# Routing of the second batch dealt out in small pieces between the shared FFN tiles, and its last tables among the expert slots

## The chip, the cores and the metric

The kernel runs on one core of a Trainium2 chip. The metric is the device time of one execution in microseconds (us), less is better. TensorE is the matrix engine (PE in the profile), VectorE is DVE, ScalarE is ACT, GpSimd is POOL, and SyncE (SP) issues most of the plain transfers.

## What is computed

One decoder layer in float32 over 32 sequences of 64 tokens, 2048 tokens of 256 features: linear attention, cross attention over a context, and a feed-forward part with 8 experts of which each token takes 2, beside a shared expert. Each has a layer norm before it and is added to x. The attention parts end before the stretch of this case; the feed-forward part is:

```python
logits = einsum('td,ed->te', xf, gate_w)
weights, indices = top_k(softmax(logits), 2)
weights = weights / weights.sum(-1, keepdims=True)
combine = einsum('tk,tke->te', weights, one_hot(indices, 8))
h = silu(einsum('td,edh->teh', xf, w_gate)) * einsum('td,edh->teh', xf, w_up)     # hidden size 176
out = einsum('teh,ehd,te->td', h, w_down, combine)
sh = silu(xf @ shw_gate) * (xf @ shw_up) @ shw_down                               # hidden size 352
out = out + sigmoid(xf @ shgate_w)[:, None] * sh
```

## The kernel before

Tokens are worked in 16 tiles of 128. A loop over the tiles carries both attention parts, the third layer norm and the router's logits. Behind it come three stages, all written out by hand in the order in which each engine does them; semaphores tie the engines together and nothing reorders.

*Shared tiles.* For tile t, TensorE turns the normalised input (transpose_sx), makes gate and up products (shared_gate, shared_up, six products each, since every float32 product is made of three passes on high and low parts), and later the transpose of the hidden row (transpose_sh, for tile t - 1) and the down product (shared_down, for tile t - 2). ScalarE makes the high part of the turned input (s_xh, L1214), the tanh of the gate (s_th, L1219) and the high part of the turned hidden row (s_hh, L1224 and L1225). VectorE makes (tanh + 1) * gate (s_gg, L1702), the low part of the *next* tile's input (s_xl, L1695), the hidden row s_h (L1709), its low part s_hl (L1718, L1720) and adds the down product to x (residual3, L1725). In VectorE's shared(t) they stand in this order, so the next tile's gate product hangs on s_gg of this one. Twelve tiles (EARLY_SHARED) are done before the experts and four behind them; the first three are mixed with the end of the attention.

*Routing.* It is done in two batches, tiles 0 to 10 and 11 to 15, called batch 1 and batch 2 here (0 and 1 in the code). VectorE finds the first choice (route_first, seven instructions), ScalarE takes the exponential (route_exp, L1134) and the shared gate's sigmoid (shared_gates), VectorE finds the second choice (route_rest, route_second), TensorE counts with a triangular and a full matrix of ones who comes before whom (ranks, four short products, L777), VectorE makes each token's row number (route_rows, L1563 to L1571) and its two weights (route_weights, L1547 to L1550), then where each expert's rows end (clear_rows, slot_counts) and a table of which expert and which first row each slot has (slot_table, L1607 to L1618). GpSimd's send scatters each token's row twice into a buffer in memory, xs_rows, sorted by expert; it waits for the row numbers of its batch and, tile by tile, for s_h of an earlier tile.

Each of these VectorE instructions is wrapped in chained(), which makes the next one wait for it.

*Expert slots.* The buffer is worked in 39 slots of 128 rows: 15 (FULL_SLOTS) that the first batch alone fills, and 24 whose table needs both batches. SyncE loads a slot's rows (load_slots) when the table of its part and that part's sends are there and slot i - 4 has been turned and given its output row numbers; TensorE reads the expert's number into a register (expert_of) and makes gate and up (gate_up), the transpose of the hidden row (L987), that of a later slot's input (L972) and down (expert_down). ScalarE and VectorE work as for shared tiles: e_th (L1283), e_gg (L1799), e_h (L1805), e_hl (L1810), xl (L1794). GpSimd scatters the results to y_rows, and at the end they are loaded, summed and stored.

VectorE's order around the change, before:

```python
            slot_table(0)
            shared(3)
            keep_logits(15)
            route_first(1)
            shared(4)
            route_rest(1)
            route_second(1)
            shared(5)
            route_rows(1)
            route_weights(1)
            clear_rows()
            shared(6)
            slot_counts(1)
            shared(7)
            slot_table(1)
```

## Time and profile before

| | |
|---|---|
| median of 3 runs | 391.13 us (389.28 to 392.36) |
| profiled execution, its own time | 389.04 us |
| its span, first to last instruction | 387.2 us |
| TensorE products, busy | 351.5 us (91%) |
| VectorE busy | 281.7 us (73%) |
| ScalarE busy | 219.5 us (57%) |
| GpSimd busy | 220.8 us (57%) |
| mean granted TensorE clock | 0.983 of full speed |

The profile is that of one execution, and its times count from the span's start. Products are pipelined and overlap, so their recorded lengths add to more than the time they take: the start of one against the start of the next tells what it costs. The shared tiles stand from about 205 to 272 us, the slots from there to 362.

### The profile page before, as it was taken

Reading aid. Unit: us, or ns where it says so; the run is one execution under the profiler, and the core shown is the slowest. Engines: PE = TensorE matmul, PEld = TensorE weight load, DVE = VectorE, ACT = ScalarE, POOL = GpSimd, SP = SyncE. Lnnn points to the kernel's source line nnn. Section 1 sums busy time; section 2 is a strip of 40 time slices with the busy share of each in tenths; the row PEclk is TensorE's granted clock in tenths of the full one; section 3 lists DMA queues with packets and bytes.
Section 4 is the critical chain, followed back from the end, with each engine's and each line's share of the span. In section 5 each row is a group of like instructions: output and inputs, shape, how many; then the busy total and the mean of one; then the engine's idle time right before and its main releaser. Section 6 shows DMA issues by size and latency. Waiting matters only on the chain.

```text
span 387.2 us, 12001 instructions
## 1 busy us (share of the span) xinstructions
PE 351.5 (91%) x3890; PEld 310.1 (80%) x3890; DVE 281.7 (73%) x922; ACT 219.5 (57%) x570; POOL 220.8 (57%) x262
## 2 busy tenths in 40 slices
PE   7789999999999999999986987998899999999971
PEld 5567778888888888888875876987788999999960
DVE  3757887788878888787886576985666767676574
ACT  3345677677776777767755333323355666665541
POOL 1247677876778766787656643544334444443362
PEclk9999999999999999999999699999999999999996
DMA  8922012211122201220000111214355343442297
GB/s 231 372 88 60 18 47 60 62 42 36 46 59 59 59 16 43 59 59 15 2 3 29 42 57 42 71 69 140 112 168 154 118 133 118 130 123 87 65 391 251
DMA packets 22013, 36.15 MB, mean 93 GB/s; under 512 B 2928, under 2 KB 15856, under 8 KB 21968
## 3 DMA queue, kind: packets, MB, share of 16 engines
q1 hardware_dynamic: 17984, 25.46, 21.6%
q0 software_dynamic: 3408, 9.39, 6.4%
q10 hardware_dynamic: 576, 0.72, 0.7%
q8 instruction: 25, 0.41, 0.4%
q14 instruction: 20, 0.16, 0.2%
HBM read 22.88 MB, written 12.69 MB: 92 GB/s over the span
## 4 chain that ended last, share of the span: by engine, by line
PE 61%; DVE 14%; ACT 9%; issue 6%; DMA 5%; another core or an unknown queue 1%; SPq 1%; POOL 1%; ACTq 1%; DVEq 0%; POOLq 0%
PE ps L851 22%; PE ps L748 4%; PE ps L666 3%; PE ps L695 3%; PE ps L720 3%; PE ps L628 3%; DMA yg<-y_rows 3%; PE ps L653 2%; PE ps L611 2%; PE ps L685 2%; PE ps L987 2%; PE ps L972 2%; ACT w_hi L1113 2%; PE ps L618 2%; ACT q L1064 2%
## 5 line engine op out<-in xcount | busy, mean ns | idle before, releaser
L578 POOL DMA_INDIRECT y_rows<-e_y,out_row x39 | 37.5, 962 | 48.2 <-ACT e_y L1294 46.1
L521 POOL DMA_INDIRECT xs_rows<-x_send,pos x32 | 31.2, 974 | 32.3 <-DVE s_h L1709 18.2
L504 POOL TENSOR_TENSOR w_lo<-w_stage,w_hi 128x852 f32 (+1 forms) x14 | 28.0, 2000 | 19.8 <-ACT w_hi L1113 18.7
L490 POOL TENSOR_TENSOR bias_t<-alibi,key_off 128x1024 f32<-128x1024 f32 x16 | 34.3, 2143 | 0.0
L497 POOL TENSOR_TENSOR sc<-sc,smax 128x1024 f32<-128x1024 f32 x16 | 30.5, 1905 | 6.6 <-DVE smax L1451 6.6
L1799 DVE SCALAR_TENSOR_TENSOR e_gg<-e_th,ps 128x176 f32<-128x176 f32 x39 | 13.2, 338 | 25.5 <-ACT e_th L1283 23.3
L851 PE MATMUL ps<-w_hi,xh 128*128 x78 | 27.2, 349 | 1.0 <-issue 0.5
L463 POOL TENSOR_TENSOR st<-mv,eps 128x1 f32<-128x1 f32 x32 | 7.0, 218 | 36.4 <-DVE mv L1434 23.5
L851 PE MATMUL ps<-w_hi,e_hh 88*128 x78 | 25.2, 323 | 1.0 <-DVE e_hl L1810 1.0
L851 PE MATMUL ps<-w_hi,s_xh 128*128 128x352 f32 x64 | 23.1, 361 | 3.0 <-DVE s_xl L1695 2.9
L1283 ACT ACTIVATE e_th<-ps 128x176 f32<-128x176 f32 x39 | 12.4, 318 | 23.2 <-PE ps L851 20.0
L851 PE MATMUL ps<-w_lo,xh 128*128 x78 | 25.2, 323 | 0.0
L851 PE MATMUL ps<-w_hi,xl 128*128 x78 | 25.2, 323 | 0.0
L1294 ACT ACTIVATE e_y<-ps,id_w 128x256 f32<-128x256 f32 x39 | 18.6, 476 | 11.2 <-PE ps L851 9.5
L851 PE MATMUL ps<-w_lo,e_hh 88*128 x78 | 21.9, 280 | 0.0
L851 PE MATMUL ps<-w_hi,e_hl 88*128 x78 | 21.9, 280 | 0.0
L1445 DVE TENSOR_TENSOR sc<-ps,bias_t 128x1024 f32<-128x1024 f32 x16 | 19.5, 1219 | 2.2 <-remote 2.2
L851 PE MATMUL ps<-w_hi,s_xl 128*128 128x352 f32 x64 | 21.0, 328 | 0.0
L851 PE MATMUL ps<-w_lo,s_xh 128*128 128x352 f32 x64 | 21.0, 328 | 0.0
L748 PE MATMUL ps<-xw_last,o2T 128*128 128x256 f32 x64 | 18.9, 420 | 2.0 <-ACT o2T L1095 0.6
L1451 DVE TENSOR_REDUCE smax<-sc 128x16 f32<-128x1024 f32 x16 | 19.5, 1220 | 0.5
L1219 ACT ACTIVATE s_th<-ps 128x352 f32<-128x352 f32 x16 | 7.4, 461 | 21.4 <-PE ps L851 16.4
(234 smaller groups left out, 1203.7 us busy)
## 6 DMA issues: line engine op xcount, KB each, us to landing
w_stage<-in_w_ffn_dram SPq DMA_DIRECT2D x14, 426.0 KB, 3.4
xs<-xs_rows SPq DMA_DIRECT2D x39, 130.5 KB
yg<-y_rows SPq DMA_DIRECT2D x8, 512.0 KB, 7.6
ctxT<-in_ctxT_dram SPq DMA_DIRECT2D x16, 128.0 KB, 2.1
out_dram<-x_all SPq DMA_DIRECT2D x7, 256.0 KB, 4.5
x_all<-in_x_dram SPq DMA_DIRECT2D x1, 1280.0 KB, 11.0
xs_rows<-zeros SPq DMA_DIRECT2D x9, 130.5 KB, 6.9
y_rows<-e_y,out_row POOLq DMA_INDIRECT x39
```

Source lines behind the costliest of these rows:

```text
L490: nc.gpsimd.tensor_tensor(bias_t[:, :].rearrange("p (h k) -> p h k", h=HEADS), alibi[:, :].rearrange("p (h k) -> p h k", h=HEADS), ko, ALU ...
L497: nc.gpsimd.tensor_tensor(v, v, spread(smax[:, :].rearrange("p (h o) -> p h o", o=1), 2, S), ALU.subtract).then_inc(sm["sub_ready"], 1)
L504: nc.gpsimd.tensor_tensor(w_lo[:, cols], w_stage[:, half, :], w_hi[:, cols].bitcast(F32), ALU.subtract).then_inc(sm["w_lo_ready"], 1)
L521: nc.gpsimd.indirect_dma_start(out=xs_d[:, :], out_offset=bass.IndirectOffsetOnAxis(ap=pos[:, t, r:r + 1], axis=0), in_=x_send[:, t, :], i ...
L578: nc.gpsimd.indirect_dma_start(out=y_d[:, :], out_offset=bass.IndirectOffsetOnAxis(ap=out_row[:, i:i + 1], axis=0), in_=e_y[:, q, :], in_o ...
L748: mm = T.matmul(ps[:, A3, 0:D], o2T[:, k, :], xwo[:, k, :], start=(k == 0), stop=(k == KC - 1))
L851: mm = T.matmul(out_ap, lhs, rhs[rows, cols], start=st, stop=en)
L1283: A.activation(e_th[:, p, :], ps[:, EG + p, 0:H], ACT.Tanh, scale=0.5).then_inc(sm["e_th_ready"], 1)
L1294: A.activation(e_y[:, q, :], ps[:, ED + q % 2, 0:D], ACT.Copy, scale=id_w[:, i, 1:2]).then_inc(sm["e_y_ready"], 1)
L1445: V.tensor_tensor(sc[:, :].rearrange("p (j c) -> p j c", j=4), ps[:, B0:B3 + 1, 0:256], bias_t[:, :].rearrange("p (j c) -> p j c", j=4), A ...
L1451: V.tensor_reduce(smax[:, :], sc[:, :].rearrange("p (h k) -> p h k", h=HEADS), AX.X, ALU.max).then_inc(sm["smax_ready"], 1)
L1799: V.scalar_tensor_tensor(out=e_gg[:, p, :], in0=e_th[:, p, :], scalar=1.0, in1=ps[:, EG + p, 0:H], op0=ALU.add, op1=ALU.mult).then_inc(sm[ ...
```

## The change

On VectorE the routing of batch 2 is dealt out in ten pieces instead of five. Four functions are cut in two: route_first gives off route_hot (the last three instructions), route_rows gives off rows_before (the first three), slot_counts gives off slot_jumps (the last two, three in batch 2), slot_table gives off slot_rows (the last four, five in batch 2). The pieces stand one between each two shared tiles, and the last three behind expert slots 4, 6 and 8. For batch 1 the pieces stand together as they did, but for slot_rows(0), which goes behind shared(3). On ScalarE route_exp(1) and shared_gates(1) move from ahead of shared(4) to behind shared(6), on TensorE ranks(1) from tile 5's end to tile 8's. No instruction is added or dropped.

```diff
@@ TensorE, shared tiles
-                if t == DRAIN_SHARED + 2:
+                if t == 8:
                     ranks(1)
@@ ScalarE
             shared_x_high(4, 0)
-            route_exp(1)
-            shared_gates(1)
             for t in range(DRAIN_SHARED + 1, EARLY_SHARED):
                 shared(t, DRAIN_SHARED, EARLY_SHARED)
+                if t == 6:
+                    route_exp(1)
+                    shared_gates(1)
@@ VectorE, the cut of route_first as an example of the four
                 chained(V.tensor_reduce(top_e, is_top, AX.X, ALU.max))
+
+            def route_hot(b):
+
+                T, n = tiles_of(b)
+                top, top_e = choice(b, "top"), choice(b, "top_e")
                 chained(V.tensor_tensor(hot[:, 0, T, :], by_expert(top_e), by_tile(rev8[:, :], n), ALU.is_equal))
@@ VectorE, shared tiles
             slot_table(0)
             shared(3)
             keep_logits(15)
+            slot_rows(0)
+            shared(4)
             route_first(1)
-            shared(4)
+            shared(5)
+            route_hot(1)
+            shared(6)
             route_rest(1)
             route_second(1)
-            shared(5)
+            shared(7)
+            route_weights(1)
+            shared(8)
+            rows_before(1)
+            shared(9)
             route_rows(1)
-            route_weights(1)
             clear_rows()
-            shared(6)
+            shared(10)
             slot_counts(1)
-            shared(7)
-            slot_table(1)
-            for t in range(8, EARLY_SHARED):
-                shared(t)
+            shared(11)
             v.wait_ge(sm["sg4_ready"], 2)
@@ VectorE, expert slots
             for i in range(1, SLOT_TILES):
                 experts(i)
+                if i == 4:
+                    slot_jumps(1)
+                if i == 6:
+                    slot_table(1)
+                if i == 8:
+                    slot_rows(1)
```

In the rows below, line numbers are each kernel's own: in the changed one s_gg is L1724, s_xl L1717, s_h L1731, e_gg L1827, e_h L1833, and the routing lines lie 1 to 21 further down.

VectorE around shared tile 3, before (ge, row_jump, row and row_i are table 0's second half, lg is keep_logits(15), tops and row_x open batch 2's first choice):

```order
L1610 TENSOR_SCALAR slot_rev<-slot_e 128x15
L1611 TENSOR_TENSOR ge<-ge,jump 128x120
L1612 TENSOR_REDUCE row_jump<-ge 128x15
L1616 SCALAR_TENSOR_TENSOR row<-consts,row_jump 128x15
L1618 TENSOR_SCALAR row_i<-row 1x15
L1702 SCALAR_TENSOR_TENSOR s_gg<-s_th,ps 128x352
L1695 TENSOR_TENSOR s_xl<-ps,s_xh 128x256
L1709 SCALAR_TENSOR_TENSOR s_h<-s_gg,sg,ps 128x352
L1485 COPY lg<-ps 128x9
L1518 TENSOR_REDUCE tops<-lg 128x5
L1519 TENSOR_TENSOR row_x<-lg,tops 128x40
L1520 TENSOR_TENSOR row_x<-row_x,consts 128x40
```

The same place in the changed kernel:

```order
L1625 TENSOR_SCALAR slot_rev<-slot_e 128x15
L1724 SCALAR_TENSOR_TENSOR s_gg<-s_th,ps 128x352
L1717 TENSOR_TENSOR s_xl<-ps,s_xh 128x256
L1731 SCALAR_TENSOR_TENSOR s_h<-s_gg,sg,ps 128x352
L1486 COPY lg<-ps 128x9
L1632 TENSOR_TENSOR ge<-ge,jump 128x120
L1633 TENSOR_REDUCE row_jump<-ge 128x15
L1637 SCALAR_TENSOR_TENSOR row<-consts,row_jump 128x15
L1639 TENSOR_SCALAR row_i<-row 1x15
L1724 SCALAR_TENSOR_TENSOR s_gg<-s_th,ps 128x352
L1717 TENSOR_TENSOR s_xl<-ps,s_xh 128x256
L1731 SCALAR_TENSOR_TENSOR s_h<-s_gg,sg,ps 128x352
```

The second half of the table now stands behind s_h of tile 3, and tile 4's s_gg comes next instead of batch 2's first choice.

ScalarE ahead of tile 4's tanh, before (L1134 is the exponential of batch 2, sgt and sg the shared gate):

```order
L1122 ACTIVATE xn3T<-ps 128x256
L1214 ACTIVATE s_xh<-ps 128x256
L1134 ACTIVATE pe<-lgs 128x40
L1141 ACTIVATE sgt<-lg 128x5
L1143 ACTIVATE sg<-sgt,quarter 128x5
L1219 ACTIVATE s_th<-ps 128x352
```

And in the changed kernel:

```order
L1122 ACTIVATE xn3T<-ps 128x256
L1214 ACTIVATE s_xh<-ps 128x256
L1219 ACTIVATE s_th<-ps 128x352
L1214 ACTIVATE s_xh<-ps 128x256
L1224 ACTIVATE s_hh<-ps 128x256
L1225 ACTIVATE s_hh<-ps 96x128
L1219 ACTIVATE s_th<-ps 128x352
```

The tanh of tile 4 stands directly behind the input copy of tile 4; the three routing instructions come three tiles later.

VectorE behind expert slot 4 in the changed kernel (before, e_gg of slot 5 follows second at once):

```order
L1838 TENSOR_TENSOR e_hl<-ps,e_hh 88x256
L1822 TENSOR_TENSOR xl<-ps,xh 128x256
L1845 TENSOR_TENSOR second<-xs,slot_rev 128x1
L1602 SCALAR_TENSOR_TENSOR cum<-ones,til 128x8
L1603 SCALAR_TENSOR_TENSOR jump<-til,consts 128x8
L1606 SCALAR_TENSOR_TENSOR jump<-taken_step,jump 128x8
L1827 SCALAR_TENSOR_TENSOR e_gg<-e_th,ps 128x176
```

Three small instructions of batch 2 now stand between slot 4's last work and slot 5's first; four and five more stand likewise behind slots 6 and 8.

## Rows read from the trace of the kernel before

A timeline row reads: start us, us, engine, line, operation, out<-in, forms, count, and in brackets the engine's idle time before it with its releaser.

**Rows 1.** The chain that ended last, routing stretch: start us, us, engine, name, line

```profile
238.76 1.25 issue
240.01 0.34 DVE s_gg L1702
```

**Rows 2.** TensorE's timeline, first gate product of shared tiles 4, 5, 9, 10

```profile
236.81 0.43 PE L851 MATMUL ps<-w_hi,s_xh 128*128 128x352 f32 x1 [0.65 <-DVE s_xl L1695]
...
240.93 0.43 PE L851 MATMUL ps<-w_hi,s_xh 128*128 128x352 f32 x1 [1.38 <-DVE s_xl L1695]
...
256.98 0.43 PE L851 MATMUL ps<-w_hi,s_xh 128*128 128x352 f32 x1 [0.70 <-DVE s_xl L1695]
...
260.62 0.33 PE L851 MATMUL ps<-w_hi,s_xh 128*128 128x352 f32 x1
```

**Rows 3.** VectorE's timeline, 234.9 to 258.8 us: where each piece of routing begins and ends

```profile
234.98 0.28 DVE L1611 TENSOR_TENSOR ge<-ge,jump 128x120 f32<-128x120 f32 x1
...
235.91 0.51 DVE L1702 SCALAR_TENSOR_TENSOR s_gg<-s_th,ps 128x352 f32<-128x352 f32 x1
...
237.35 0.20 DVE L1518 TENSOR_REDUCE tops<-lg 128x5 f32<-128x40 f32 x1
...
241.81 0.18 DVE L1530 SCALAR_TENSOR_TENSOR pe<-hot,pe 128x40 f32<-128x40 bf16 x1
...
243.07 0.52 DVE L1702 SCALAR_TENSOR_TENSOR s_gg<-s_th,ps 128x352 f32<-128x352 f32 x1
...
245.19 0.16 DVE L1563 COPY counts<-upto 128x8 f32<-128x8 f32 x1
...
246.79 0.16 DVE L1547 TENSOR_SCALAR tops<-tops 128x5 f32<-128x5 f32 x1
...
247.57 0.50 DVE L1702 SCALAR_TENSOR_TENSOR s_gg<-s_th,ps 128x352 f32<-128x352 f32 x1
...
249.69 0.41 DVE L1581 TENSOR_SCALAR cnt_i<-upto 128x8 int32<-128x8 f32 x1
...
250.95 0.18 DVE L1587 TENSOR_TENSOR_SCAN cum<-ones,til 128x8 f32<-128x8 f32 x1
...
251.57 0.52 DVE L1702 SCALAR_TENSOR_TENSOR s_gg<-s_th,ps 128x352 f32<-128x352 f32 x1
...
253.69 0.34 DVE L1607 TENSOR_TENSOR ge<-consts,cum 128x192 f32<-128x192 f32 x1
...
254.77 0.36 DVE L1611 TENSOR_TENSOR ge<-ge,jump 128x192 f32<-128x192 f32 x1
...
256.07 0.51 DVE L1702 SCALAR_TENSOR_TENSOR s_gg<-s_th,ps 128x352 f32<-128x352 f32 x1
...
258.74 0.52 DVE L1702 SCALAR_TENSOR_TENSOR s_gg<-s_th,ps 128x352 f32<-128x352 f32 x1 [0.47 <-ACT s_th L1219]
```

**Rows 4.** ScalarE's timeline, copy of tile 4 and the exponential of batch 2

```profile
235.15 0.38 ACT L1214 ACTIVATE s_xh<-ps 128x256 fp32r<-128x256 f32 x1
238.96 0.24 ACT L1134 ACTIVATE pe<-lgs 128x40 f32<-128x40 f32 x1 [3.43 <-DVE lgs L1524]
```

**Rows 5.** Windows, one expert slot: length, then PE, PEld, DVE, ACT, POOL busy, PEclk

```profile
288.35:290.45 2.10, 2.10 (x18) 2.06 (x17) 1.51 (x7) 1.34 (x5) 0.81 (x2) 1.00 0.61 190
```

**Rows 6.** VectorE's and TensorE's timelines, h of slot 5 and its transpose

```profile
286.48 0.33 DVE L1805 SCALAR_TENSOR_TENSOR e_h<-e_gg,ps 128x176 f32<-128x176 f32 x1
...
287.80 0.38 PE L987 MATMUL ps<-ident,e_h 128*88 128x128 f32 x2
```

**Rows 7.** VectorE's and ScalarE's timelines, end of the shared tiles

```profile
269.36 0.42 DVE L1725 TENSOR_TENSOR x_all<-ps,x_all 128x256 f32<-128x256 f32 x1 [1.25 <-PE ps L851]
...
269.41 0.39 ACT L1278 ACTIVATE xh<-ps 128x256 fp32r<-128x256 f32 x1 [1.95 <-PE ps L972]
```

**Rows 8.** TensorE's timeline at 213 us, and the window behind it (columns of rows 5)

```profile
213.27 0.41 PE L756 MATMUL ps<-ident,xn 128*128 128x128 f32 x2 [3.21 <-DVE sc L1445]
...
215.00:220.00 5.00, 5.00 (x19) 4.64 (x20) 2.00 (x7) 1.06 (x1) 4.29 (x6) 0.50 0.15 53
```

More of the change, by code:

```diff
@@ L1551, in route_weights, with rows_before @@
                                 ).then_inc(sm["fields_ready"], 1)
-            def route_rows(b):
+            def rows_before(b):
                 T, n = tiles_of(b)
@@ L1557, in route_rows @@
                 ranks = ps[:, RANKS[b], :]
-                in_tile, row = rows_scratch(b, "in_tile"), rows_scratch(b, "row")
+                in_tile = rows_scratch(b, "in_tile")
                 by_tiles = in_tile.rearrange("p (e t) -> p e t", e=NE)
@@ L1566, in route_rows @@
                                              not_first[b][:, :, :].rearrange("p e t -> p (e t)"), in_tile, 0.0, ALU.mult, ALU.add))
+            def route_rows(b):
+                T, n = tiles_of(b)
+                counted = n * NE
+                ranks, row = ps[:, RANKS[b], :], rows_scratch(b, "row")
                 chained(V.tensor_tensor(row.rearrange("p (t e) -> p t e", e=NE), ranks[:, 0:counted].rearrange("p (t e) -> p t e", e=NE),
@@ L1610, in slot_table, with slot_rows @@
                 chained(V.tensor_scalar(slot_rev[:, I], slot_e[:, 0:n], -1.0, float(NE), ALU.mult, ALU.add))
+            def slot_rows(b):
+                i0, n = ((0, FULL_SLOTS), (FULL_SLOTS, SLOT_TILES - FULL_SLOTS))[b]
+                I = slice(i0, i0 + n)
+                iota, g = iota_slot[:, 0:n], ge[:, 0:n, :]
                 chained(V.tensor_tensor(g, g, by_tile(jump[:, :], n), ALU.mult))
@@ L1642, in body @@
                     route_first(0)
+                    route_hot(0)
                 if has(t, 0):
@@ L1738, in _ @@
             shared_x_low(0, 0)
+            rows_before(0)
             route_rows(0)
@@ L1759, in _ @@
             slot_counts(0)
+            slot_jumps(0)
             sh_low(1, 1, A2)
```

1 line of the change is left out of this document (added).

## The prediction

> **What bounds the kernel now.** I read the page first, for which engine is busy and the granted clock, then the chain that ended last to see where the end is not held by TensorE, then the timelines of TensorE and VectorE side by side there, and last the windows by expert slot.
>
> Over most of the span TensorE sets the end. The exception that this change touches is the shared FFN with the routing of batch 2. There the chain runs instruction by instruction through VectorE, and TensorE comes in only now and then; between batch 2's first routing piece and the next shared tile it shows 1.25 us in which VectorE waits [rows 1]. The first gate product of a shared tile marks when TensorE begins it. Tile 4 begins at 236.81, tile 5 at 240.93, tile 9 at 256.98, tile 10 at 260.62 [rows 2]. From 9 to 10, with no routing between, a tile takes 3.64 us and TensorE has no gap: that is its own pace, gate, up, down and transposes together. Tile 4 took 4.12 though it has no down product yet, and tiles 5 to 8 together 256.98 - 240.93 = 16.05, which is 1.49 more than four times 3.64. Each marked gap waits for s_xl, the low part of the next tile's input, which VectorE makes behind s_gg of the current tile.
>
> What stands ahead of those s_gg is the routing. On VectorE the second half of table 0 runs from 234.98 to 235.91, batch 2's first choice from 237.35 until ScalarE gets its input at 238.96 [rows 4], the second choice from 241.81 to 243.07, ranks, rows and weights from 245.19 to 247.57, the counts with their jumps from 249.69 to 251.57, the table from 253.69 to 256.07 [rows 3]. VectorE's own work on a tile is 256.07 to 258.74 less the 0.47 it waited, 2.20 us [rows 3]. A tile of 3.64 thus leaves VectorE 1.44 us. The table alone is 2.38 us, the ranks with the weights 2.38, the counts with the jumps 1.88: too long for one gap, and TensorE waits for the rest.
>
> **Where it is hidden and where not.** Two lengths say how large a piece may be. s_gg of tile 9 begins 1.76 after tile 9's first product (258.74 - 256.98), and the next tile's first product comes 0.90 after s_gg begins (236.81 - 235.91), so the chain product, tanh, s_gg, s_xl, product closes in 2.66 us. Against 3.64 that is 0.98 of play for one late piece, and the 1.44 bounds what may come in every gap.
>
> **The change, part by part.**
>
> 1. Table 0's second half (four instructions, 0.93 us) moves from ahead of shared tile 3 to behind it. s_gg of tile 3 can begin 0.93 earlier. ScalarE's copy for tile 4 ends at 235.15 + 0.38 = 235.53 [rows 4]; s_xl follows, and TensorE can begin tile 4 0.47 after that if the 0.43 between s_gg and s_xl is taken off 0.90. That gives 236.00 instead of 236.81: gain 0.8, between 0 and 0.93. What reads the moved half is the load of slot 0, and that also waits until the first batch is sent, whose last send waits for s_h of tile 8; so the delay costs nothing.
>
> 2. The first choice is cut in two, and the exponential moves on ScalarE from ahead of the tanh of tile 4 to behind tile 6. Before, that tanh stood behind an exponential that waited 3.43 us for lgs [rows 4], which is the 1.25 us of rows 1. Without it tile 4 has the closed chain of 2.66 us instead of 4.12: gain 1.46. The lower bound is 4.12 - 3.64 = 0.48, should tile 4 go at the pace of the others; I take 1.46, since there is no down product in it. What is late next is TensorE itself.
>
> 3. The rest is dealt out one piece to a gap. By the starts in rows 3: ranks with their rows 1.60 (now in two gaps, about 0.7 and 0.9), weights 0.78 with the end rows, second choice 1.26, counts without the jumps 1.26. Every one is under 1.44, so tiles 5 to 8 should fall to TensorE's pace: gain 1.49, less about 0.1 (an estimate) for the four short rank products, which stay in the stretch, now behind tile 6's down product. The bounds are 0 and 1.49. The rank products wait for nothing any more: the one-hot rows are ready two tiles earlier in the new order. Behind them on TensorE stands tile 9's gate, and VectorE's ranks piece comes behind shared tile 8, so a wait there would need them over a tile late.
>
> 4. Behind it: the row numbers of batch 2 (pos) now come after tile 9 instead of after tile 5. GpSimd's sends of tile 11 wait for s_h of tile 9 anyway, and now also for the rows piece, about 1 us behind it. Its two sends have a tile of 3.64 for themselves. No cost. The clearing of the ends needs them only among the slots.
>
> 5. Among the expert slots: three instructions behind slot 4 (0.62), then the nine of the table, four behind slot 6 and five behind slot 8 (by that share about 1.1 and 1.3), 3.00 in all [rows 3]. A slot takes 2.10 us, and VectorE is busy 1.51 of it [rows 5]: 0.59 free. h of slot 5 is done at 286.48 + 0.33 = 286.81 and its transpose on TensorE begins at 287.80 [rows 6], 0.99 later. So a piece of up to 0.59 + 0.99 = 1.58 us is hidden once, if the next slots give it back at 0.59 each; the largest is 1.30, and two slots lie between the pieces. The last one is close, since not all of the piece before it may have been given back. Bounds 0 and 3.00 us; I take 0.15, near the rows that show it hidden. Nobody waits for the table itself: the first load of a slot of the second part waits for the row numbers of slot 11, which VectorE makes behind all three pieces, and TensorE reads the slot's expert later still.
>
> The sum against the profiled execution: 0.8 + 1.46 + 1.39 = 3.65 gained, 0.15 given back, 3.5 us. That execution took 389.04 with a span of 387.2, and would take 385.5. From slot 0 on TensorE sets the end, so what it arrives earlier is kept. The median of the three runs is 391.13, 2.1 over the profiled one; I take the difference over to the median: 391.13 - 3.5 = 387.6 us. All bounds taken against me, 0.48 is left of the gain in the tiles and 3.00 is paid in the slots: 2.5 slower; all for me, 0.93 + 1.46 + 1.49 = 3.9 faster.
>
> **The rivals.**
>
> *The pieces cost in full among the slots.* If TensorE is tied among the slots to e_gg, the counterpart of s_gg, the 3.00 us stand in its way: gain 3.65 - 3.00 = 0.65, 390.5 us. For it: VectorE has only 0.59 us free a slot against 1.44 in a shared tile. Against it: the 0.99 us by which h is early.
>
> *A late signal goes or comes.* At the end of the shared tiles VectorE and ScalarE go on within 0.05 us of each other, at 269.36 and 269.41, after 1.25 and 1.95 us of waiting for TensorE products whose recorded end is 1.4 us earlier [rows 7]. If that stall belongs to a place in the program it stays. If it belongs to what else happens to move at that time, shifting everything by 3.5 us can remove it: 1.4 more gained, 386.2 us. It can as well come up elsewhere. On fetching of instructions the Trainium skill, "Runtime: NRT & Kernel Launch", section "Instruction fetch mechanics", says that an engine draws its instructions ahead in blocks and that crossing from one to the next is mostly hidden. By that rule the stall is no property of the place and might go, which is the 386.2; the trace doesn't say which it is.
>
> *A burst meets a stall and the clock falls* (the slower side). Earlier in the trace TensorE idled 3.21 us, and in the 5 us behind the granted clock was 0.50, the 1.2 GHz level [rows 8]. If one of the pieces behind slots 4, 6 or 8 meets a stall like that of rows 7, the two add: 1.3 + 1.95 is about as long an idle time. It would cost that 3.2 and half of 5 us at the lower level, 5.7 in all: 5.7 - 3.65 = 2.1 slower, 393.2 us. It decides from the point where TensorE stands idle for some 3 us at once.
>
> **How the numbers follow.** The forecast has 0.61, the pieces paid in full 0.20, the vanished signal 0.13, the fallen clock 0.06. The range goes from 385.2, below the vanished signal's time, to 390.8, just past the pieces paid in full; it leaves out most of the clock case and the tails. 1% is 3.9 us, about what a measurement of this kernel tells from no change (the three runs lie within 0.8%). The forecast lies just short of that bound, so I give 0.28 of its 0.61 to faster by over 1%, and nearly all of the vanished signal's: 0.40. Slower by over 1% is a corner of the clock case, 0.03. Within 1% is the rest, 0.57.
>
> **What would show it.** Right: first gate products of tiles 5 to 9 about 3.64 us apart, tile 9's at 253.3 or so in place of 256.98; no wait for s_xl at TensorE in those tiles; the tanh of tile 4 behind its own gate product and not behind the exponential; slots 5 to 10 at 2.1 to 2.4 us each as before, and slot 0's first product 3.6 earlier. Wrong: a gap at TensorE behind slot 8 that ends with e_h or e_hl, a rank product that waits for hot, GpSimd's sends of batch 2 holding up the loads from slot 15 on, or tiles that stay above 3.7 us with VectorE never idle, which would mean that a piece costs more than its start-to-start time.

## The result, and the profile after

In the first comparison the changed kernel took **392.21 us** (median of 13 runs, 389.33 to 394.06) beside 389.92 us for the kernel before (13 runs, 388.40 to 392.36). The ratio is **1.0053, 95% interval 1.0031 to 1.0074**: 0.5% slower, where the prediction had 387.6 us. By the bound of 1% this is no change; the time lies above the predicted range. The profiled execution took 390.13 us, the second fastest of the 13, and the slower executions have the lower mean clock (389.33 us with 0.978 of full speed, 394.06 with 0.964). So the trace shows 1.1 us of the difference in span, where the medians differ by 2.3. Three executions of later comparisons (399.31 us, 485.55 and 659.75) were in a slow state: they count in the medians printed here, but not in the ratios.

Three lines of the page of the changed kernel, first comparison: the span, the clock granted to TensorE in 40 slices, and the chain that ended last by engine.

```profile
span 388.3 us, 12003 instructions
...
PEclk9999999999999999999999799998999999999995
...
PE 68%; ACT 9%; DVE 7%; issue 7%; DMA 3%; another core or an unknown queue 3%; POOL 2%; DVEq 0%; ACTq 0%; POOLq 0%; SPq 0%
```

There is a second dip in the clock row (slice 28), and 3% of the chain is put down to "another core", though this program has one core. Both matter below. TensorE's timeline of the same execution (start, duration, engine, line, operation; in brackets the idle time before and its releaser) answers to [rows 2]: the first gate products of tiles 4, 5, 8, 9 and 10, then the transposes of slots 0 and 1, the down product of shared tile 10, and slot 0's first product.

```profile
234.95 0.43 PE L851 MATMUL ps<-w_hi,s_xh 128*128 128x352 f32 x1
...
237.62 0.43 PE L851 MATMUL ps<-w_hi,s_xh 128*128 128x352 f32 x1
...
249.62 0.43 PE L851 MATMUL ps<-w_hi,s_xh 128*128 128x352 f32 x1 [1.10 <-DVE s_xl L1717]
...
253.38 0.41 PE L851 MATMUL ps<-w_hi,s_xh 128*128 128x352 f32 x1
...
257.63 0.43 PE L851 MATMUL ps<-w_hi,s_xh 128*128 128x352 f32 x1 [0.46 <-DVE s_xl L1717]
...
264.60 0.60 PE L972 MATMUL ps<-ident,xs 128*128 128x128 f32 x4
...
269.77 0.46 PE L851 MATMUL ps<-w_hi,s_hh 128*128 128x256 f32 x1 [4.57 <-DVE x_all L1747]
...
272.23 0.64 PE L851 MATMUL ps<-w_hi,xh 128*128 x1
```

Tile 4 takes 2.67 us as forecast (2.66), and tile 9 begins at 253.38 instead of 256.98, 3.6 us earlier, as forecast. The sum agrees better than its terms: tiles 5 to 8 take 15.76 us here in place of 16.05, a gain of 0.29 where 1.39 was forecast, and tile 4 begins 1.86 earlier where 0.8 was. Later TensorE stands idle for 4.57 us, and slot 0 begins at 272.23, where it was 271.32 in the kernel before: everything that was won is lost there, and 0.9 us more. The same down product in the kernel before:

```profile
269.94 0.36 PE L851 MATMUL ps<-w_hi,s_hh 128*128 128x256 f32 x1 [1.56 <-DVE x_all L1725]
```

The idle time is 3.01 us longer in the changed kernel. From that product to slot 0 it takes 2.46 us instead of 1.38. VectorE's and ScalarE's timelines answer to [rows 7]. VectorE:

```profile
264.95 0.58 DVE L1731 SCALAR_TENSOR_TENSOR s_h<-s_gg,sg,ps 128x352 f32<-128x352 f32 x1 [1.43 <-PE ps L851]
...
269.20 0.42 DVE L1747 TENSOR_TENSOR x_all<-ps,x_all 128x256 f32<-128x256 f32 x1 [1.70 <-remote]
```

ScalarE:

```profile
262.44 0.47 ACT L1219 ACTIVATE s_th<-ps 128x352 f32<-128x352 f32 x1 [1.50 <-issue]
266.31 0.39 ACT L1224 ACTIVATE s_hh<-ps 128x256 fp32r<-128x256 f32 x1 [3.40 <-remote]
...
269.25 0.66 ACT L1279 ACTIVATE xh<-ps 128x256 fp32r<-128x256 f32 x2 [2.39 <-remote]
```

xh at 269.25 reads the transposes that began at 264.60 and had ended by 265.20: 4.05 us late. x_all at 269.20 reads a down product that ended at 264.76, 4.44 us late. ScalarE and VectorE go on within 0.05 us of each other, as they did in [rows 7], where the lateness was 1.4 us. "remote" says that the trace holds no event of this core that released them. I call such a case a late signal. That is a name for the row and not a cause: the ends of products are modelled in the profile, so the trace doesn't tell a signal that was late from a product that was. In this trace there are five such episodes behind 230 us (at 240, 247, 255, 264 to 269 and 278 to 280 us) against three in the kernel before (262, 268 to 271 and 277 to 280). Behind the longest of them the clock falls. Windows of the changed kernel (columns of [rows 5]):

```profile
266.00:268.00 2.00, 0.00 (x0) 0.00 (x0) 0.61 (x2) 0.54 (x2) 1.70 (x2) 1.00 0.31 111
...
270.00:272.00 2.00, 2.00 (x11) 2.00 (x11) 0.64 (x5) 0.00 (x0) 0.00 (x0) 0.50 0.00 0
272.00:274.00 2.00, 2.00 (x10) 1.76 (x9) 1.18 (x5) 0.58 (x3) 0.00 (x0) 0.68 0.00 0
```

The granted clock is 0.50, the 1.2 GHz level, in 270 to 272 and partly in 272 to 274: as in [rows 8], after TensorE had stood idle. That is why the stretch from the down product to slot 0 is 1.08 us longer. From slot 0 to the gate products of the last slot the changed kernel loses 1.3 us more (359.14 against 356.92). What GpSimd does in those microseconds is six sends, 0.30 to 0.47 us of pause between them; the first and the last:

```profile
260.56 0.96 POOL L521 DMA_INDIRECT xs_rows<-x_send,pos  x1 [5.18 <-issue]
...
267.07 0.96 POOL L521 DMA_INDIRECT xs_rows<-x_send,pos  x1 [0.30 <-issue]
```

They are one row because batch 2's row numbers come only behind tile 9 now (the prediction's step 4). In both traces each episode behind 230 us went with four or more sends 1.3 to 1.6 us apart; the episode at 209 to 213 us went with two. That rows of sends make signals late was my first theory, called A in the expectations.

### The profile page after: what moved, and what is told of

Same layout as the page of the kernel before. It is cut to its first block, busy times and chain, and to the rows that moved or that the text cites. A ratio compares the mean times of both kernels' runs of the same rounds, so it can differ in the third digit from the quotient of the medians.

```text
span 388.3 us, 12003 instructions
## 1 busy us (share of the span) xinstructions
PE 353.5 (91%) x3890; PEld 312.3 (80%) x3890; DVE 281.3 (72%) x922; ACT 219.4 (56%) x570; POOL 221.2 (57%) x262
## 4 chain that ended last, share of the span: by engine, by line
PE 68%; ACT 9%; DVE 7%; issue 7%; DMA 3%; another core or an unknown queue 3%; POOL 2%; DVEq 0%; ACTq 0%; POOLq 0%; SPq 0%
PE ps L851 25%; PE ps L748 4%; PE ps L666 4%; PE ps L720 4%; PE ps L695 3%; PE ps L628 3%; PE ps L611 3%; PE ps L653 2%; PE ps L685 2%; PE ps L987 2%; PE ps L972 2%; PE ps L618 2%; PE ps L615 2%; ACT w_hi L1113 2%
## 5 line engine op out<-in xcount | busy, mean ns | idle before, releaser
L1827 DVE SCALAR_TENSOR_TENSOR e_gg<-e_th,ps 128x176 f32<-128x176 f32 x39 | 13.2, 338 | 22.9 <-ACT e_th L1284 18.4
L851 PE MATMUL ps<-w_hi,s_hh 128*128 128x256 f32 (+1 forms) x48 | 16.4, 341 | 6.9 <-DVE x_all L1747 6.0
```

Source lines behind the costliest of these rows:

```text
L851: mm = T.matmul(out_ap, lhs, rhs[rows, cols], start=st, stop=en)
L1827: V.scalar_tensor_tensor(out=e_gg[:, p, :], in0=e_th[:, p, :], scalar=1.0, in1=ps[:, EG + p, 0:H], op0=ALU.add, op1=ALU.mult).then_inc(sm[ ...
```

## The experiments

The experiments ran in six comparisons, each with the kernel before on the same chip. They name their chips: 11 (the first four runs), 12 (the next four), 10 (two comparisons), 2 and 4 (the stalls). The first comparison names none, so I can't say whether its chip was one of these at another hour.

### Four tests of the sends

**The kernel before with its sends bunched.** The odd tiles' sends wait for one h more:

```diff
-                    pool.wait_ge(sm["s_h_ready"], t - 1)
+                    pool.wait_ge(sm["s_h_ready"], t if t % 2 and t < 10 else t - 1)
```

> The kernel before, with one edit: GpSimd's two sends of an even tile (from tile 5 on) wait as before, those of an odd tile for one s_h more, so that the four sends of two tiles come in one row. Theory A (a row of four or more sends, 1.27 us apart, goes with TensorE signals that reach ScalarE and VectorE 1 to 4 us late; what was won in the changed kernel was lost so): new late signals near the end of each row in the shared tiles, 1 to 2 us of idle TensorE for each, 2 to 6 us slower than before. Rival B (the late signals belong to something else, instruction fetching or the place in the program): late signals stay at 263 and 268 us as in the kernel before and none are added; within 1 us of before. Rival C (the loss in the changed kernel is VectorE's routing pieces): within 1 us of before as well.

**The kernel before with sends spaced.** In send(), inside the loop over the two rows:

```diff
                        in_=x_send[:, t, :], in_offset=None).then_inc(sm[f"sent{b}"], 16)
+                    if t >= 4:
+                        nc.gpsimd.tensor_tensor(pad[:, 2 * t + r:2 * t + r + 1], eps[:, :], neg_half[:, :], ALU.pow)
```

> The kernel before, with a small GpSimd operation of 0.57 us on a spare buffer behind each send from tile 4 on: sends are at least about 1.9 us apart instead of 1.27. Theory A (rows of sends make the late signals): the late signals of 263, 268 to 270.8 and 277 to 280 us go; 1 to 3 us faster than before, or the lateness shrinks with the spacing. Rival B (not the sends): they stay, and the time with them, within 1 us. A middle result (rows at 1.9 us still bring some) would show as smaller lateness at the same places.

**The changed kernel with the same edit.**

> The changed kernel with the same small GpSimd operation behind each send. Theory A: the late signals at 240, 247, 255 and 264 to 269 us go or shrink, tiles 5 to 11 stay at 3.64 us, slot 0 starts about 3 us earlier than before, no clock at half speed near 270 us; 3 to 5 us faster than the changed kernel and 1 to 4 us faster than before. Rival B (not the sends): as the changed kernel, 2 us slower than before, with the idle 4.6 us in front of slot 0. Rival D (the pieces among the slots are paid in full, 3 us): the shared tiles gain, but the slots from 5 on take 3 us more than before, sum within 1 us of before.

**The changed kernel with batch 2's row numbers one tile earlier:**

```diff
-                if t == 8:
+                if t == 7:
                     ranks(1)
...
             route_weights(1)
-            shared(8)
             rows_before(1)
-            shared(9)
+            shared(8)
             route_rows(1)
             clear_rows()
+            shared(9)
             shared(10)
```

> The changed kernel with the rank products one tile earlier and the pieces behind them as well, so that the row numbers of batch 2 are there one tile earlier; the pieces behind shared tile 7 are two then. Theory A: the sends of tiles 11 to 13 come no longer six in a row but in pairs or fours, the idle 4.6 us in front of slot 0 shrinks to 1 to 2 us and the clock does not fall behind it: 2 to 4 us faster than the changed kernel. Rival B (not the sends): no difference to the changed kernel but that of a larger piece behind tile 7, 0 to 0.5 us slower.

Measured: 1.0082 (1.0055 to 1.0110), 1.0023 (1.0001 to 1.0046), 0.9973 (0.9949 to 0.9997) and 0.9893 (0.9865 to 0.9922), all against the kernel before, which took 383.68 us here and not 389.92. The first of the four did more than I meant: in its trace ten sends stand in one row. GpSimd's timeline of the kernel with bunched sends, the first and the last of the ten:

```profile
253.72 0.95 POOL L521 DMA_INDIRECT xs_rows<-x_send,pos  x1 [3.73 <-DVE s_h L1709]
...
265.06 0.96 POOL L521 DMA_INDIRECT xs_rows<-x_send,pos  x1 [0.30 <-issue]
```

and ScalarE's, in the midst of them:

```profile
259.32 0.38 ACT L1224 ACTIVATE s_hh<-ps 128x256 fp32r<-128x256 f32 x1 [0.77 <-PE ps L893]
...
261.37 0.47 ACT L1219 ACTIVATE s_th<-ps 128x352 f32<-128x352 f32 x1 [1.50 <-PE ps L851]
```

s_hh is in time behind its transposes, with the same 0.77 us of waiting as in quiet tiles, and s_th follows its gate product in 0.04 us. So theory A as I had stated it is refuted on this chip: rows of sends don't make late signals by themselves. None of these four traces has a late signal among the shared tiles. The bunched kernel is 0.8% slower, within what theory A had forecast, but for another and plainer reason: its sends come later, and TensorE waits for rows of slots 0 and 1 (0.59 and 0.87 us, released by the DMA of xs). The spacing costs something too (the third run is 3 us above the unspaced kernel of the next comparison) and cures nothing, since here nothing is late. What these runs say of a chip with late signals is nothing.

### Both kernels again, unchanged

> The kernel before, unchanged, for a profile from the chip of this comparison (the earlier profiles of both kernels may come from another). Theory E (the late TensorE signals belong to the chip or to the hour, not to the order of the program): if this chip shows none, the span is some 381 to 382 us, 5 below the 387.2 of the first profile, and the difference lies at 209 to 212, 262 to 271 and 277 to 280 us. Theory A (rows of sends make them): late signals at the rows of four sends, as in the first profile.

> The changed kernel, unchanged, on the chip of this comparison. Theory E: without late signals the change gives what its steps promise, 3 to 4 us (the variant with the row numbers a tile earlier gave 4.2), gate products of tiles 5 to 11 3.64 us apart, slot 0 some 3.5 us earlier, no half clock near 270 us. Theory A: slower than before by 2 us, with rows of four to six sends and late signals behind them, the idle 4.6 us and the half clock, as in its first profile. Rival F (the row numbers of batch 2 come too late and this costs by itself): 2 to 4 us slower than the variant with them a tile early, and no late signal seen.

The kernel before against itself: 383.83 us, 1.0001 (0.9982 to 1.0020). The changed kernel: **379.90 us, ratio 0.9889 (0.9865 to 0.9913)**. A third copy on another chip gave 379.34 us and 0.9885 (0.9857 to 0.9912):

> The changed kernel unchanged, to tell what kind of chip this comparison ran on. Theory E (what turns the sign is the chip: one with late signals or one without): before near 383.7 us goes with a ratio of about 0.989, before near 390 us with one of about 1.005, and nothing between. Were the first verdict a chance of the kernel's own scatter instead, the ratio would fall between these.

Theory E holds as far as it could be tried: before at 383.6 to 384.1 us goes with a change that is 1.1% faster. Its other half, before near 390 us with a ratio of 1.005, is the first comparison alone. TensorE's timeline of the kernel before on this chip (first gate products of tiles 4, 5 and 9, and slot 0's first product):

```profile
233.65 0.43 PE L851 MATMUL ps<-w_hi,s_xh 128*128 128x352 f32 x1 [0.64 <-DVE s_xl L1695]
...
237.76 0.43 PE L851 MATMUL ps<-w_hi,s_xh 128*128 128x352 f32 x1 [1.37 <-DVE s_xl L1695]
...
253.82 0.43 PE L851 MATMUL ps<-w_hi,s_xh 128*128 128x352 f32 x1 [0.70 <-DVE s_xl L1695]
...
266.54 0.41 PE L851 MATMUL ps<-w_hi,xh 128*128 x1
```

and of the changed kernel (tiles 4, 5, 6, 9 and 10, then the down product that was 4.57 us late in the first trace, and slot 0's first product):

```profile
232.63 0.43 PE L851 MATMUL ps<-w_hi,s_xh 128*128 128x352 f32 x1
...
235.31 0.43 PE L851 MATMUL ps<-w_hi,s_xh 128*128 128x352 f32 x1
...
238.97 0.33 PE L851 MATMUL ps<-w_hi,s_xh 128*128 128x352 f32 x1
...
249.71 0.41 PE L851 MATMUL ps<-w_hi,s_xh 128*128 128x352 f32 x1
...
253.35 0.33 PE L851 MATMUL ps<-w_hi,s_xh 128*128 128x352 f32 x1
...
261.03 0.36 PE L851 MATMUL ps<-w_hi,s_hh 128*128 128x256 f32 x1 [0.20 <-DVE x_all L1747]
...
262.41 0.41 PE L851 MATMUL ps<-w_hi,xh 128*128 x1
```

The idle time in front of the down product is 0.20 us in place of 4.57. Side by side, changed minus before:

| place | first comparison | chip 12 |
|---|---|---|
| tile 4 begins | 234.95 - 236.81 = -1.9 | 232.63 - 233.65 = -1.0 |
| tile 9 begins | 253.38 - 256.98 = -3.6 | 249.71 - 253.82 = -4.1 |
| slot 0 begins | 272.23 - 271.32 = **+0.9** | 262.41 - 266.54 = **-4.1** |
| span | 388.3 - 387.2 = +1.1 | 378.6 - 383.3 = -4.7 |

The profiled execution of the kernel before took 385.22 us here, 1.4 over its median, so the span row overstates the gain; the medians give 3.8. Read along a kernel, the first comparison is ahead of chip 12 up to the first send at 209 us, by 0.9 us in the kernel before and 1.2 in the changed one; from there it is late. The kernel before is 3.2 us later at tile 4 and 4.8 at slot 0; the changed one is 2.3 us later at tile 4, 3.7 at tile 9 and 9.8 at slot 0. This also explains [rows 8]: the idle time of 3.21 us with the half clock behind it was itself a late signal. In the traces of chip 12 the same product waits 1.04 us, and the window behind it has full clock. The clock doesn't hang on this idle time alone, though: in three other traces (the kernel before with spaced sends, the changed one with its row numbers a tile earlier, and the second run of paired sends) the same wait is 1.02 to 1.03 us, and the granted clock is 0.50 from 214 to 216 us. The window of the changed kernel on chip 12:

```profile
214.00:219.00 5.00, 4.45 (x33) 4.14 (x31) 3.28 (x11) 2.27 (x4) 3.79 (x6) 1.00 0.15 53
```

In this execution of the changed kernel the six sends of tiles 11 to 13 stand in one row as well, from 255.65 to 262.93, and ScalarE's timeline shows no harm from them:

```profile
260.64 0.66 ACT L1279 ACTIVATE xh<-ps 128x256 fp32r<-128x256 f32 x2 [0.74 <-PE ps L972]
```

The same instruction had come 4.05 us late in the first trace.

### The prediction's steps one by one

**Pieces among the slots undone** (jumps and table of batch 2 behind tile 10, slot rows behind tile 11, nothing among the slots):

```diff
             slot_counts(1)
+            slot_jumps(1)
+            slot_table(1)
             shared(11)
+            slot_rows(1)
...
-                if i == 4:
-                    slot_jumps(1)
-                if i == 6:
-                    slot_table(1)
-                if i == 8:
-                    slot_rows(1)
```

> The changed kernel with the pieces among the expert slots put back: jumps and table of batch 2 behind shared tile 10, its slot rows behind tile 11, nothing among the slots. By the prediction's step 5 the pieces among the slots cost 0.15 (0 to 3.0): then this is equal to the changed kernel or 0 to 1 us slower, as the table's 2.4 us stands in the way of the last shared tiles. Rival D (paid in full among the slots): 1 to 3 us faster than the changed kernel.

379.99 us, 0.9902 (0.9872 to 0.9931), beside 379.90 for the changed kernel: no difference. From slot 0 to slot 11 it takes 26.85 us where the changed kernel takes 27.04, but its slot 0 begins at 263.89, 1.5 later. The 0.19 us is no price of the pieces. Two traces of the changed kernel differ by more (27.04 and 26.59), and in this one the clock fell at slot 0:

```profile
262.24 0.36 PE L851 MATMUL ps<-w_hi,s_hh 128*128 128x256 f32 x1 [1.84 <-DVE x_all L1747]
...
264.00:266.00 2.00, 2.00 (x7) 2.00 (x8) 1.39 (x7) 0.45 (x2) 0.00 (x0) 0.50 0.18 67
```

Slot 0 took 3.77 us with it in place of 2.85. What can be said is that the pieces cost far less than the 3.00 us that they are long: slots 5 to 9, among which they stand, take 11.49 and 11.69 us in two traces of the changed kernel, 12.44 with the pieces undone and 12.00 in the kernel before.

**Large pieces kept, steps 1 and 2 alone:**

```diff
-            route_first(1)
-            shared(5)
-            route_hot(1)
-            shared(6)
...
+            route_first(1)
+            route_hot(1)
+            shared(5)
+            route_rest(1)
+            route_second(1)
+            shared(6)
...
```

(and so on: ranks, rows and weights behind tile 6, counts and jumps behind 7, the whole table behind 8; the exponential at tile 5).

> The changed kernel with steps 1 and 2 kept (table 0's second half behind tile 3, the exponential off tile 4's way) and step 3 and 5 undone: batch 2's routing behind tiles 4 to 8 in the old large pieces, nothing among the slots. By the prediction's sum: 0.8 + 1.46 stay, 1.4 of the tiles is lost: 2.2 us faster than before (ratio 0.994) where no signal is late; first gate products of tiles 5 to 10 above 3.64 us apart, by the length of the piece. Were the gain one of fewer waits for signals rather than of piece size, it would be near the 3.8 us of the whole change. On a chip like that of the first two profiles (before at 389 to 390 us) theory A lets the rows of sends decide: the sends of tile 11 come earlier here than in the change, so 1 to 3 us faster than before.

381.37 us, 0.9917 (0.9886 to 0.9948): 3.2 us faster than before with a wide interval, where 2.2 was expected; the clock time can't separate these. The trace does: tile 4 takes 2.68 us as in the change, and tiles 5 to 9 take 3.64, 3.71, 4.12, 4.01 and 4.50, so together they take 1.9 us more than the changed kernel's 18.04. In the shared tiles the pieces' size and place are worth that.

**Batch 2's routing one tile earlier all through** (a try for something better):

```diff
+            slot_counts(1)
             shared(10)
-            slot_counts(1)
+            slot_jumps(1)
             shared(11)
...
-                if i == 4:
-                    slot_jumps(1)
-                if i == 6:
+                if i == 4:
                     slot_table(1)
-                if i == 8:
+                if i == 6:
                     slot_rows(1)
```

(on top of the fourth run above).

> The changed kernel with batch 2's routing one tile earlier all through: weights and end rows behind tile 7, row numbers behind tile 8, counts behind 9, jumps behind 10; among the slots only the table behind slot 4 and the slot rows behind slot 6. It aims at the gap in front of slot 11, 3.3 us in the changed kernel where its neighbours take 2.1 to 2.3 (the first slot whose rows wait for batch 2). If that gap hangs on the sends and slot rows of batch 2: it falls to 2.2 to 2.5 us, 0.5 to 1.5 us faster than the changed kernel, ratio to before 0.985 to 0.989. If it hangs on something else: as the changed kernel, within 0.5 us, or up to 1 us slower where a piece no longer fits. On a chip like that of the first two profiles (before at 389 to 390 us) theory A expects it 2 to 4 us faster than the changed kernel, since no six sends come in a row.

379.07 us, 0.9872 (0.9841 to 0.9904), beside 379.34 us for the changed kernel in the same comparison: no difference that can be measured. The gap in front of slot 11 (3.29 us in the changed kernel of chip 12) stayed at 3.25 here, and in the third copy of the changed kernel it was 2.78. TensorE's row at slot 11 in the changed kernel of chip 12 names the DMA of the slot's rows:

```profile
287.92 0.44 PE L972 MATMUL ps<-ident,xs 128*128 128x128 f32 x2 [0.32 <-DMA xs<-xs_rows]
```

so there TensorE waits for the load. That the slot rows are what holds the load up isn't shown: two slots earlier they changed nothing. The gap was 2.20 us in the first of the stalls below, with VectorE's order unchanged. What sets it stays open.

**Earlier rows and spaced sends together**, and **pairs of sends kept apart** (two small operations behind each pair instead of one behind each send), the latter on two chips:

> The changed kernel with both edits: row numbers of batch 2 one tile earlier, and the small GpSimd operation behind each send. If spacing the sends and the earlier rows help apart from each other: 1 us or more below the variant with the earlier rows alone (ratio to before about 0.986). If the spacing only costs GpSimd time where no signal is late: 0 to 1 us above it (0.989 to 0.992).

> The changed kernel with two small GpSimd operations (0.57 us each) behind each pair of sends from tile 4 on: pairs stay at 1.27 us, but no more than two sends are in a row. On a chip like that of the runs before this one (before at 383.7 us, no late signals): 0 to 2 us slower than the changed kernel, as in the variant with one operation behind each send, since GpSimd gets later with batch 2. On a chip like that of the first two profiles (before at 389 to 390 us): theory A expects the late signals of 240, 247, 255 and 264 to 269 us gone and 3 us or more off the changed kernel; if they stay, rows of sends are not what makes them there either.

> The changed kernel with pairs of sends kept apart, as in the run before with this name's pairs. Where before takes about 384 us and no signal is late: a ratio of 0.992 as there. Where before takes about 390 us, theory A: a ratio of 0.985 to 0.995 instead of the 1.005 of the changed kernel, late signals at 240, 247, 255 and 264 to 269 us gone. If the ratio is 1.00 or more and they stay: rows of sends do not make them.

0.9962 (0.9942 to 0.9983), 0.9918 (0.9880 to 0.9955) and 0.9962 (0.9930 to 0.9993). On chips where nothing is late the spacing costs 1 to 3 us, more than I had expected in the first and the last of the three; it was to cure what these chips don't have.

### What an idle time in front of slot 0 costs

No comparison met a chip with late signals again, so I made the idle time in the changed kernel, with N small activations ahead of ScalarE's copy of the h of tile 10:

```diff
+                if t == 11:
+                    for j in range(N):
+                        A.activation(pad[:, j:j + 1], quarter[:, :], ACT.Copy)
                 if t - 1 >= first:
                     sh_high(t - 1, (t - 1) % 2)
```

> The changed kernel with nine small activations (some 0.2 us each, 1.8 in all) ahead of ScalarE's copy of the h of shared tile 10, so that TensorE stands idle in front of slot 0 for about 2 us more. If an idle time there is paid once and nothing more: 1.5 to 2 us slower than the changed kernel, clock at full speed behind it. If part of it is hidden by the 3.3 us gap in front of slot 11: 0.5 to 1.5.

> The same with twenty activations, some 4 us, near the 4.57 us that TensorE idled there in the first trace of the changed kernel. By the third rival of the prediction (an idle time of some 3 us or more and the clock falls): 4 us and 1 to 2.5 us on top for a stretch at half clock behind it, 5 to 6.5 us slower than the changed kernel, which is slower than before by 1 to 2.5 us: the first result of the changed kernel from this one stall. If the clock stays: 3 to 4 us slower than the changed kernel, as fast as before within 1 us.

379.44 us (0.9901, 0.9880 to 0.9922) and 380.62 us (0.9920, 0.9880 to 0.9961): nearly nothing, because I had the length wrong. ScalarE's timeline of the second of them:

```profile
257.70 1.96 ACT L1236 ACTIVATE pad<-quarter 128x1 f32<-128x1 f32 x20
```

Twenty activations took 1.96 us, 0.1 each. They held ScalarE up by 2 us, but TensorE stood idle for 1.12 us in place of 0.20, and slot 0 began at 262.60, between the 262.41 and 262.68 of the unchanged kernel. So this stall is hidden but for some tenths of a microsecond (380.62 beside 379.90 on chip 12, and 379.44 with nine activations on the same chip). With N = 50:

> The changed kernel with fifty of the small activations ahead of ScalarE's copy of the h of shared tile 10: 4.9 us by the 0.1 us that one took in the stall of twenty (1.96 us), of which some 0.8 lies beside other work, so that TensorE idles about 4 us in front of slot 0. With the third rival of the prediction: 4 us for the idle time and 1 to 2.5 us for half a clock behind it, 5 to 6.5 us slower than the changed kernel, 384.5 to 386.5 us where before takes 383.7. If the clock stays at its full level: 3.5 to 4 us slower, 383 to 384 us.

**385.52 us, ratio 1.0064 (1.0040 to 1.0088)**: 5.6 us above the changed kernel's 379.90 (6.7 by the two ratios), and slower than before. TensorE's timeline:

```profile
259.66 0.60 PE L973 MATMUL ps<-ident,xs 128*128 128x128 f32 x4
264.18 0.55 PE L852 MATMUL ps<-w_hi,s_hh 128*128 128x256 f32 x1 [3.92 <-DVE x_all L1751]
```

and the windows of this kernel:

```profile
262.00:264.00 2.00, 0.00 (x0) 0.00 (x0) 0.92 (x4) 1.58 (x11) 0.36 (x1) 0.63 0.19 69
264.00:266.00 2.00, 1.82 (x8) 1.86 (x9) 0.83 (x5) 0.00 (x0) 0.00 (x0) 0.50 0.00 0
266.00:268.00 2.00, 2.00 (x10) 1.99 (x9) 0.73 (x2) 0.54 (x2) 0.00 (x0) 0.50 0.00 0
268.00:270.00 2.00, 2.00 (x12) 2.00 (x12) 1.37 (x8) 0.32 (x1) 0.00 (x0) 0.67 0.00 0
```

The picture of the first trace comes back: an idle time of 3.92 us (4.57 there), the granted clock falling while TensorE stands idle (0.63 in 262 to 264) and at 0.50 from 264 to 268, and a ratio of 1.0064 (1.0053 there). Slot 0 begins at 266.73, which is 4.3 us later than on chip 12: the down product begins 3.15 later (264.18 and 261.03), and from it to slot 0 it takes 2.55 us instead of 1.38 at the lower clock. Slot 0 itself takes 3.42 instead of 2.85. The medians, 5.6 us apart, come from two chips, and the executions of this kernel scatter from 383.44 (the profiled one) to 385.99, so I take the price as 4 to 7 us, most of it idle time in the profiled execution.

## Why the prediction was right and wrong

**Steps 1 to 3, right in mechanism and near in size.** On chip 12, where no signal is late:

| step | predicted | measured, and from what |
|---|---|---|
| 1, table 0's half behind tile 3 | 0.8 | 0.8: tile 4 is 1.02 earlier, of which 0.25 stood already at tile 3's up product |
| 2, first choice cut, exponential moved | 1.46 | 1.43: tile 4 takes 2.68 instead of 4.11 |
| 3, pieces in the gaps | 1.39 | 1.66: tiles 5 to 8 take 14.40 instead of 16.06 |
| 5, pieces among the slots | -0.15 | too small to measure: 379.90 with them, 379.99 without |
| whole, by the medians | 3.5 | 3.8 and 4.5 (379.90 beside 383.69, 379.34 beside 383.84) |

Step 3 is the larger one since tiles 5 to 8 fall a little under the 3.64 us that I took for TensorE's pace (3.66, 3.54, 3.55 and 3.65) and the rank products cost nothing to be seen. In the first comparison the 3.6 us at tile 9 look like the forecast, but in part by luck: step 2 gave its 1.45, step 3 only 0.29 of 1.39, since the gate's signal of one of these tiles was late (TensorE idle for 1.10 us at 249.62), and tile 4 was 1.86 earlier, of which 0.56 stood already at 213 us (212.71 in place of 213.27), ahead of anything that was changed.

**Step 4, "No cost", right in the time and wrong in how.** I had the wait for the rows piece as 1 us and gave the two sends of tile 11 a tile to themselves. In fact the rows piece ends at 254.8 on chip 12 and the sends of tiles 11, 12 and 13 stand in one row of six. Where signals are in time this costs nothing that shows: from slot 0 to slot 11 the changed kernel takes 27.04 us, the kernel before 27.68. In the first comparison the longest late signal lies at this row.

**What failed is the step from the tiles to slot 0: "From slot 0 on TensorE sets the end, so what it arrives earlier is kept", in a sum that takes for granted that the gain arrives there.** The sum has no term for a longer wait in front of slot 0. The transposes ahead of it began 3.18 us earlier than before (264.60 and 267.78), and all of it was lost in front of slot 0, 3.01 us in the longer idle time (4.57 in place of 1.56) and 1.08 with the clock at half behind it. The prediction had both parts. Its second rival took the stall of [rows 7] for something that could go or come, but priced only its going, 1.4 us; the coming got half a sentence. Its third rival had the right mechanism and nearly the right price: a stall as in [rows 7] makes TensorE stand idle for over 3 us, the clock falls as in [rows 8], 5.7 us in all, 393.2 us. The stall made by hand cost 5.6 us by the medians, and the first comparison's ratio times the 391.13 us shown ahead of the prediction gives 393.2. That the totals agree so well is luck: the rival put 2.5 us on the clock, where the two traces show 1.1 and 1.2 up to slot 0. The place was another (in front of slot 0, not behind slots 4, 6 or 8), no routing piece was part of it, and the chance of 0.06 was far too small. I had let it depend on a routing piece meeting a stall; but the stall needs no partner, since late signals of 1.4 to 1.9 us were in the profile in several places, and nothing in it bounded their length.

I could have read more from the profile of before. Its late signals weren't one stall at one place: the 3.21 us of idle time at 213 us [rows 8] came from one too, and I took it only as an example of what the clock does. A rival with a chance of a fifth or more for the slower side would have been in order.

The prediction named a rule for the late signal of [rows 7]. On chip 12 that stall is gone, with the kernel before unchanged, so it isn't a property of the place in the program; whether instruction fetching had any part in it on the first chip no run shows. The Trainium skill, "Runtime: NRT & Kernel Launch", section "Instruction fetch mechanics", has it that crossing from one block of instructions to the next is mostly hidden. The traces of the other chips agree: the same instructions show no wait of this kind there.

**What is shown and what isn't.** Shown: on chips 12 and 10 the change is 1.1% faster, and so is its near variant on chip 11 (0.9893); an idle time of 3.9 us in front of slot 0 alone turns this into 0.6% slower, with the clock fallen. So one such idle time is enough for the first result; the other late signals of that trace weren't rebuilt. Not shown: what makes signals late in the first comparison. That the late signals and the rows of sends coincide there in both traces is a correlation; on five chips up to ten sends in a row did nothing, so they aren't enough. They may be needed beside something that the first chip had: nothing was late ahead of the first send. The first two traces also lack semaphore events, and these too are missing only behind the first send (below), so the two may well have one cause. That something held up the signals, or that the recording itself did, are rivals that no run tells apart. Whether spaced sends would have helped on that chip could not be tried, since no comparison met it again.

## To carry to other kernels

A wait whose product has long ended by the trace is no property of its place. Where a profile shows such waits, take their size from the longest one, give a change that runs into them the price of an idle time and a fallen clock, and don't let a few good microseconds of forecast hang on one chip: a second chip tells more than ten more runs on the first, whose 13 runs gave an interval clear of 1 and had the sign wrong for the others. And time that is won ahead of a stretch is safe only if the engine arrives there with its signals in time; here ScalarE could stand 2 us at the seam with TensorE idle for 1.1 and nearly nothing lost, and an idle time of 3.9 us cost more than the whole change had won.

## What the runs showed of the hardware

- The same kernel took 389.92 us in the first comparison and 383.6 to 384.1 us in the six others, 1.6% apart, at nearly the same granted clock (0.983 and 0.986 in the profiled executions). At GpSimd's first indirect send, at 209 us, the first comparison's trace is still 0.9 us ahead of chip 12's.
- In the first two traces ScalarE and VectorE went on up to 4.4 us after the recorded end of the TensorE product that they waited for, both engines at once, while ScalarE's signals reached VectorE in time (s_hh at 266.59 to 266.85, s_hl at 266.89). The semaphore records of these two traces have 4,554 and 4,545 events; those of the other traces 5,449 to 5,467 for nearly the same program. About a sixth is missing, and none of the others has such a loss. In the kernel before, 2,086 events lie ahead of 209 us and 2,081 on chip 12, so all that is missing lies behind the first send; of the 900, 693 are landings of transfers. The page shows it as "another core or an unknown queue": 1% of the chain in the kernel before, 3% in the changed one, and no such item on chip 12.
- Ten indirect sends of 0.96 us in a row, 1.26 us apart, delayed no signal on chip 11.
- The length of one idle time doesn't tell by itself whether TensorE's granted clock falls. With 3.92 us in front of slot 0 it stood at 0.50 from 264 to 268 us. With 1.84 us at the same place (the pieces undone) it also fell to 0.50, and with 1.56 us (the kernel before, first comparison) it stayed at 1.00. With 1.02 to 1.04 us at 212 us it stayed at 1.00 in thirteen traces and fell to 0.50 in three.
- An activation of 128x1 took 0.1 us in a row of twenty (1.96 us for all), half of what single small ones of 128x5 and 128x40 show in the timeline (0.20 and 0.23 us).
